# Graph network on one core: GpSimd multiplies out the left sides of two slots of each group, VectorE those of the other two

## The chip, the cores and the metric

The kernel runs on one core of one Trainium2 chip. The metric is the device time of the whole program in microseconds (us). The engines are TensorE (PE in the rows, PEld for its weight loads), VectorE (DVE), ScalarE (ACT), GpSimd (POOL) and SyncE (SP, which only issues DMAs).

## The reference, cut to what matters

512 nodes with 512 features pass four graph layers. The change lies in the preparation of the first, sparse attention over 8192 edges with eight heads:

```
p   = exp(q[row] . k[col] * scale + bias - m[row])      # per edge and head
out = segment_sum(p / segment_sum(p, row) * v[col], row)
```

The kernel does not gather per edge. It first builds dense tables: for each node `row`, each `col` and each head the sum of `exp(bias)` over the edges between them, and as a ninth table the number of these edges. The tables are made on TensorE as products of masks, and the attention is then dense.

## The kernel before, in words

The edges lie sorted by `dst`, in 64 tiles of 128 (an edge per partition). The destination nodes are cut into 37 blocks of 14 (`BW`). A **slot** is a tile together with a block that it meets; there is room for 100 slots (`SLOTS`), and four slots make a **group** (`GROUP`). For a slot, TensorE multiplies two things:

- the **left side**, 128 edges x 126: for each of the 14 nodes of the block and each of the nine columns (`KW`: eight heads and a one for the count) the edge's weight if it ends in that node, otherwise zero. It is `mask` (bf16, 14 wide) times `wp` (nine wide), both spread by broadcasting, and it is there twice, for a high and a low part of the weights (`a` = 0, 1). A group's left sides are 128 x 1008 numbers (4 slots x 2 parts x 126) in `st_ring`, which the rows show as `c_rounded`.
- the **one-hot**, 128 edges x 512: which node the edge comes from, `iota_f` compared with the edge's source, in `hot_ring`, which the rows show as `wide_rounded`.

Two matmuls a slot (128x126 by 128x512, line 1395) add into one of four accumulators in PSUM. `st_ring` and `hot_ring` hold `RING` = 2 groups.

Work on each engine is written out by hand in program order, and engines wait on semaphores. Groups 0 to 23 are unrolled, group 24 is a loop of `trips` rounds (one with these inputs, by the trace). Per group VectorE makes four one-hots (line 792), each waiting in `pair_mm` until TensorE has done with that slot two groups earlier, and then all left sides in one multiplication (line 798), which raises `built`. Behind some groups it also takes a finished tile of q, k or v out of PSUM (`qkv_out`, lines 817, 819, 823); behind group 3 it makes the later masks (line 757). TensorE takes group g once `built` has reached g + 1 (`pairs`), and between groups does 7, 4, 3, then ten times 2, then ten times 1 steps of the products for q, k and v (line 1377). ScalarE copies each finished block out of PSUM and clears the bank (lines 483, 488, semaphore `evacuated`). GpSimd fills constants in the first 9 us and does nothing after that.

Of the kernel before, what the change touches and what calls it, by code (L numbers as in the profile page):

```python
# [6 lines left out]
ALU = mybir.AluOpType  # L7
ACT = mybir.ActivationFunctionType
AX = mybir.AxisListType
F32 = mybir.dt.float32  # L10
# [6 lines left out]
P = 128  # L17
# [10 lines left out]
BW = 14  # L28
NBK = -(-N // BW)
KW = H + 1  # L30
# [6 lines left out]
GROUP = 4  # L37
NG = SLOTS // GROUP
RING = 2
ACC = 4  # L40
STAGES = 3
FIXED = SLOTS - GROUP
MAX_TRIPS = -(-(ET * NBK - FIXED) // GROUP)
FLOOR = -3e38
ENDS, PICK, NEEDS = 130, 200, 400
# [19 lines left out]
def gnn_kernel(nc, x, src, dst, bias, eps, cols, rows, wq, wk, wv, wo, w1_0, w2_0,  # L65
               wl_t, wr_t, w1_2, w2_2, w1_3t, w2_3t, out):
    ctx = ExitStack()
    with ctx:
# [75 lines left out]
        at, cuts = 0, {}  # L144
        for name, words in (("mask", SLOTS * BW), ("bias", HP * P), ("src", P), ("dst", P), ("low", P),
# [3 lines left out]
        mask = cuts["mask"].bitcast(BF16).rearrange("p (s a w) -> p s a w", a=2, w=BW)  # L149
# [18 lines left out]
        wp = wslot_r[:, 3, :, :].rearrange("p t n -> p (t n)")[:, 0:SLOTS * 2 * KW].rearrange(  # L168
            "p (s a k) -> p s a k", a=2, k=KW)
        st_ring = c1_r[:, :, :].rearrange("p t n -> p (t n)")[:, 0:RING * GROUP * 2 * BROWS].rearrange(  # L170
            "p (g a w k) -> p g a w k", g=RING, w=BW, k=KW)
# [42 lines left out]
        def rowp(name):  # L214
# [14 lines left out]
            "eps_column", "ln_var", "ln_std", "ln_coef", "h_ready", "z_ready",  # L229
            "bias_top", "bias_turned", "bias_column", "bias_spread", "bias_low", "lows_mm", "lows_ready", "weights_exp", "turned", "t_ready",  # L230
            "x_sums", "z_scalar", "w_hi", "pick_zeros", "meets_ready", "ranks_mm", "ranks_ready", "ends_mm", "ends_ready", "rounds_ready", "slots_ready", "slots_mm",
            "picks_ready", "rows_ready", "picks_mm", "weights_mm", "weights_read", "round_steps", "built", "pair_mm", "pair_steps",
            "evacuated", "staged", "b_out0", "b_out1", "b_out2", "c2_in", "qkv_mm",
            "qkv_ready",
            "c1_ready", "no_edge_ready", "bv_in", "b_ready", "qk_steps", "st_mm", "lows_found", "e_ready", "e_turned",
# [20 lines left out]
        LAST_V = range(3 * NT - 2, 3 * NT)  # L256
        assert qkv_group[NT * LAST_V[0] - 1] + RING < NG - 1
        chunk_w = bank[4][:, 0:H * GROUP]

        def block_parts(n):  # L260

            b = NBK - 1 - n
            if b == NBK - 1:
                return [((t, slice(TAKEN, P)), t * LEFT, LEFT) for t in range(NT)]
            first = b % BLOCKS
            return [((b // BLOCKS, slice(first, first + (BW - 1) * BLOCKS + 1, BLOCKS)), 0, BW)]
# [64 lines left out]
        @block.gpsimd  # L331
        def _(pool):
            nc.gpsimd.iota(steps[:, :], [[1, 1 + SLOTS]], base=0, channel_multiplier=0,
                           allow_small_or_imprecise_dtypes=True).then_inc(S["tables"], 1)
            nc.gpsimd.memset(ident[:, :], 0.0).then_inc(S["pool_order"], 1)
            nc.gpsimd.memset(ones[:, :], 1.0).then_inc(S["pool_order"], 1)
            pool.wait_ge(S["pool_order"], 2)
            nc.gpsimd.affine_select(out=ident[:, :], in_=ident[:, :], compare_op=ALU.not_equal, fill=1.0,
                                    base=0, pattern=[[-1, P]], channel_multiplier=1).then_inc(S["consts"], 1)

            nc.gpsimd.affine_select(out=before[:, :], in_=ones[:, :], compare_op=ALU.is_gt, fill=0.0,
                                    base=0, pattern=[[1, P]], channel_multiplier=-1).then_inc(S["consts"], 1)
            nc.gpsimd.iota(low_f, [[-BW, NBK + 1]], base=(NBK - 1) * BW, channel_multiplier=0,
                           allow_small_or_imprecise_dtypes=True).then_inc(S["tables"], 2)
            nc.gpsimd.iota(need_c[:, :], [[0, 1]], base=-NBK, channel_multiplier=1,
                           allow_small_or_imprecise_dtypes=True).then_inc(S["tables"], 1)
            nc.gpsimd.memset(pick, 0.0).then_inc(S["pick_zeros"], 1)
            nc.gpsimd.memset(wp[:, :, 0, H:].bitcast(F32), 1.0).then_inc(S["tables"], 1)
            nc.gpsimd.memset(wp[:, :, 1, H:].bitcast(F32), 0.0).then_inc(S["tables"], 1)
            pool.wait_ge(S["lows_ready"], 1)  # L350
            node_of = iota_f[:, :].rearrange("p (t c) -> p t c", t=NT)
            for t in range(NT):
                nc.gpsimd.iota(node_of[:, t, 0:TAKEN].rearrange("p (i j) -> p i j", j=BLOCKS),
                               [[1, BW], [BW, BLOCKS]], base=t * TAKEN, channel_multiplier=0,
                               allow_small_or_imprecise_dtypes=True).then_inc(S["tables"], 1)
            nc.gpsimd.iota(node_of[:, :, TAKEN:], [[LEFT, NT], [1, LEFT]], base=NT * TAKEN, channel_multiplier=0,
                           allow_small_or_imprecise_dtypes=True).then_inc(S["tables"], 1)
        @block.scalar
        def _(act):
            act.dma_start(idx_dst, dst.rearrange("(t p) -> t p", p=P)).then_inc(S["dst_in"], 16)  # L360
# [114 lines left out]
            for b in range(NBK):  # L475
# [3 lines left out]
                a = bank[(b + 1) % ACC][0:BROWS, :]  # L479
# [123 lines left out]
        def _(dve):  # L603
# [124 lines left out]
            def step(count, ins, wait=True):  # L728
                ins.then_inc(S["round_steps"], 1)
                if wait:  # L730
                    dve.wait_ge(S["round_steps"], count)
# [45 lines left out]
            whole, early = slice(0, SLOTS), slice(0, RING * GROUP)  # L777
            later, chunk = slice(RING * GROUP, SLOTS), slice(FIXED, SLOTS)
            next_masks, last_masks = slice(RING * GROUP, 6 * GROUP), slice(6 * GROUP, SLOTS)
# [7 lines left out]
            def one_hots(u, s0, ks=range(GROUP), freed=None):  # L787

                for k in ks:
                    if freed is not None:  # L790
                        dve.wait_ge(S["pair_mm"], freed + (k + 2))
                    nc.vector.tensor_scalar(hot_ring[:, u, k, :], iota_f[:, :], picked[:, 0, s0 + k:s0 + k + 1], None,  # L792
                                            ALU.is_equal)

            def left_sides(u, s0):

                c = slice(s0, s0 + GROUP)
                nc.vector.tensor_tensor(  # L798
                    st_ring[:, u, :, :, :],
                    mask[:, c, :, :].rearrange("p s a w -> p (s a) w").unsqueeze(3).broadcast_to(  # L800
                        [P, 2 * GROUP, BW, KW]),
                    wp[:, c, :, :].bitcast(F32).rearrange("p s a k -> p (s a) k").unsqueeze(2).broadcast_to(
                        [P, 2 * GROUP, BW, KW]), ALU.mult).then_inc(S["built"], 1)

            def build(g, u, s0, freed=None):

                one_hots(u, s0, freed=freed)
                left_sides(u, s0)

            def qkv_out(n):  # L810

# [36 lines left out]
            for t in (0, 1):  # L848
# [5 lines left out]
            step(8, slot_masks(next_masks))  # L854
            link(nc.vector.tensor_scalar(rounds_f[:, :], ends_row[:, NBK - 1:NBK], float(GROUP - 1 - FIXED),
                                         float(GROUP), ALU.add, ALU.max))
# [8 lines left out]
            dve.wait_ge(S["ends_ready"], 1)  # L865
            trips = dve.value_load(rounds_i[0:1, 0:1], min_val=1, max_val=MAX_TRIPS)
            for g in range(RING, NG - 1):
                build(g, g % RING, g * GROUP, (g - RING) * GROUP)
                if g == RING + 1:
                    step(9, slot_masks(last_masks))  # L870
                for n in range(LAST_V[0]):
                    if qkv_group[(n + 1) * NT - 1] + RING == g:
                        qkv_out(n)
            settle()
            with nc.vector.Fori(0, trips) as j:
                build(NG - 1, 0, FIXED, j * GROUP + (FIXED - RING * GROUP))
                at = j * 6 + 9
# [296 lines left out]
            for t in range(NT):  # L1174
                c = slice(t, t + 1)
# [13 lines left out]
        def _(pe):  # L1189
# [198 lines left out]
            def pairs(g, u, held):  # L1388

                pe.wait_ge(S["built"], g + 1)  # L1390
                for k in range(GROUP):
                    pe.wait_ge(S["evacuated"], held[k])
                    to = acc[0:BROWS, bass.ds((held[k] & (ACC - 1)) * N, N)]
                    for a in range(2):
                        last = nc.tensor.matmul(to, st_ring[:, u, 2 * k + a, :, :].rearrange("p w k -> p (w k)"),  # L1395
                                                hot_ring[:, u, k, :], start=False, stop=False, skip_group_check=True)
                    last.then_inc(S["pair_mm"], 1)
# [24 lines left out]
            for g in range(NG - 1):  # L1422
# [10 lines left out]
                if g == 2:  # L1433
                    pe.wait_ge(S["ends_ready"], 1)
                    trips = pe.value_load(rounds_i[0:1, 0:1], min_val=1, max_val=MAX_TRIPS)
            with nc.tensor.Fori(0, trips) as j:
                pe.wait_ge(S["rows_ready"], j + 1)
                pe.sem_inc(S["pair_steps"], 1)
                pairs(j + (NG - 1), 0, choices(FIXED))
                pe.wait_ge(S["qkv_ready"], LAST_V[0])  # L1440
                pair_table(j + 1, slice(FIXED, SLOTS), lambda k: qkv_step(len(qkv) - NT + k))

# [215 lines left out]
```

## Time and profile before

| what | us |
|---|---|
| median of three runs (393.72 to 393.85) | 393.78 |
| span of the profiled execution, first to last instruction | 394.1 |
| groups 0 to 24 and the q, k, v products on TensorE | 22 to 109.6 |
| TensorE busy in the whole span | 374.8 |
| VectorE busy | 312.1 |
| GpSimd busy | 4.2 |

The page gives no other time of the profiled execution than its span, which is 0.3 us above the median of the runs. Busy time counts instructions; where two of one engine overlap in the rows, the overlap counts once.

### The profile page before, as it was taken

To read this page: it belongs to the slowest core of one execution; us is meant where nothing else is said; L and a number is where in the kernel's file an instruction comes from. 1 tells how busy PE (TensorE), PEld (TensorE's weight loads), DVE (VectorE), ACT (ScalarE), POOL (GpSimd) and SP (SyncE) were. 2 spreads that over 40 slices of the span, in tenths; PEclk is the share of its full clock that TensorE was granted. 3 is DMA by queue.
4 is the path that set the end of the run, shared out by engine and by line. 5 is a ranking of instruction groups with operands and counts; after the bars stand their busy time and mean duration, and the time that the engine had idled before them with its cause. 6 is when DMAs were issued, how large, how long until landed. Compare 5 with 4: busy or idle time off the path is not lost.

```text
span 394.1 us, 5108 instructions
## 1 busy us (share of the span) xinstructions
PE 374.8 (95%) x1786; PEld 282.2 (72%) x1786; DVE 312.1 (79%) x660; ACT 171.6 (44%) x287; POOL 4.2 (1%) x19
## 2 busy tenths in 40 slices
PE   2989999999999999999999999999999999999994
PEld 1545566666657888887678788887588878787773
DVE  5889999999848789897868976698875788388236
ACT  5664666563044234244559533262363530145410
POOL 4000000000000000000000000000000000000000
PEclk9999999999999999999999999999999999999988
DMA  7602444343135000068200512200600050000002
GB/s 238 250 1 69 152 154 141 105 153 112 52 112 183 1 2 0 2 215 315 111 2 1 172 43 101 114 0 0 211 4 0 2 180 33 2 0 0 2 12 94
DMA packets 16360, 32.92 MB, mean 84 GB/s; under 512 B 1360, under 2 KB 1488, under 8 KB 16336
## 3 DMA queue, kind: packets, MB, share of 16 engines
q1 hardware_dynamic: 15744, 32.25, 23.9%
q10 hardware_dynamic: 592, 0.36, 0.3%
q8 instruction: 15, 0.25, 0.3%
q14 instruction: 9, 0.07, 0.1%
HBM read 21.07 MB, written 1.05 MB: 56 GB/s over the span
## 4 chain that ended last, share of the span: by engine, by line
PE 77%; DVE 14%; ACT 4%; issue 2%; DMA 1%; DVEq 0%; ACTq 0%
PE acc L1395 11%; PE bank L1377 10%; PE bank L1480 7%; PE bank L1270 6%; PE bank L1271 6%; PE bank L1251 4%; PE acc L1251 4%; PE acc L1271 4%; PE acc L1270 4%; PE bank L1465 3%; PE acc L1451 3%; DVE big_rounded L652 2%; PE acc L1228 2%; PE bank L1228 2%; PE acc L1545 2%
## 5 line engine op out<-in xcount | busy, mean ns | idle before, releaser
L1395 PE MATMUL acc<-wide_rounded,c_rounded 128*126 128x512 f32 x200 | 59.5, 439 | 0.7 <-ACT acc L464 0.7
L1395 PEld LDWEIGHTS acc<-wide_rounded,c_rounded 128*126 128x126 f32 x200 | 36.9, 186 | 19.8 <-issue 13.0
L792 DVE TENSOR_SCALAR wide_rounded<-iota_f,picked 128x512 fp32r<-128x512 f32 x100 | 42.2, 480 | 1.5 <-issue 1.1
L483 ACT COPY z_sb<-acc 126x512 f32<-126x512 f32 x37 | 21.6, 585 | 42.0 <-PE acc L1395 33.3
L507 ACT ACTIVATE wide<-wide,low_col 128x512 f32<-128x512 f32 x32 | 21.3, 715 | 32.9 <-DVE low_col L905 32.8
L1480 PEld LDWEIGHTS bank<-v_sb,big 128*128 128x128 f32 x256 | 29.7, 192 | 4.7 <-issue 4.0
L625 DVE TENSOR_TENSOR wslot_rounded<-wslot,wide_rounded 128x512 fp32r<-128x512 f32 x24 | 16.2, 687 | 21.2 <-ACT wslot L377 21.2
L1480 PE MATMUL bank<-v_sb,big 128*128 128x65 f32 x256 | 31.6, 277 | 0.0
L798 DVE TENSOR_TENSOR c_rounded<-row_bc,wslot_rounded 128x1008 fp32r<-128x1008 bf16 x25 | 30.0, 1201 | 0.0
L1377 PE MATMUL bank<-t_sb,wslot 128*128 128x512 f32 x64 | 29.5, 594 | 0.5 <-ACT t_sb L459 0.5
L652 DVE TENSOR_TENSOR big_rounded<-big,big_rounded 128x1024 fp32r<-128x1024 f32 x24 | 29.1, 1221 | 0.5
L369 ACT ACTIVATE std<-mv,eps_c 128x1 f32<-128x1 f32 x20 | 5.8, 290 | 41.0 <-DVE mv L657 25.9
L917 DVE TENSOR_TENSOR big<-bank,big 128x512 f32<-128x512 f32 x32 | 20.5, 682 | 0.9 <-PE bank L1465 0.9
L905 DVE CUSTOM_DVE_ANT_0 wide<-acc,t_sb 128x512 f32<-128x512 f32 x32 | 20.7, 683 | 0.2 <-DVE t_sb L893 0.2
L1377 PEld LDWEIGHTS bank<-t_sb,wslot 128*128 128x128 f32 x64 | 12.0, 189 | 11.5 <-issue 9.6
L488 ACT COPY acc<-zero_c 126x512 f32<-126x512 f32 x33 | 19.4, 588 | 1.0
L1271 PE MATMUL acc<-big_rounded,wslot_rounded 128*128 128x512 f32 x48 | 19.6, 409 | 0.0
L1270 PE MATMUL acc<-big_rounded,wide_rounded 128*128 128x512 f32 x48 | 19.4, 404 | 0.0
L1465 PE MATMUL bank<-ident,wide 128*128 128x128 f32 x128 | 17.6, 276 | 1.2 <-ACT wide L507 1.2
L1465 PEld LDWEIGHTS bank<-ident,wide 128*128 128x128 f32 x128 | 14.3, 146 | 3.1 <-ACT wide L507 2.5
L1377 PE MATMUL bank<-wslot,t_sb 128*128 128x512 f32 x32 | 16.4, 598 | 0.0
L374 ACT ACTIVATE wide_rounded<-bank,col 128x512 fp32r<-128x512 f32 x12 | 8.3, 693 | 17.4 <-PE bank L1271 17.4
(312 smaller groups left out, 769.6 us busy)
## 6 DMA issues: line engine op xcount, KB each, us to landing
big<-z_sb SPq DMA_DIRECT2D x36, 252.0 KB
big<-in_w SPq DMA_DIRECT2D x4, 2048.0 KB, 7.8
x_sb<-in_x SPq DMA_DIRECT2D x8, 256.0 KB, 4.6
big<-in_w_3t SPq DMA_DIRECT2D x2, 1024.0 KB, 6.7
row_bc<-in_rows SPq DMA_DIRECT2D x7, 256.0 KB, 6.4
wslot<-in_wq SPq DMA_DIRECT2D x1, 1024.0 KB, 8.9
wslot<-in_wk SPq DMA_DIRECT2D x1, 1024.0 KB, 10.7
wslot<-in_wv SPq DMA_DIRECT2D x1, 1024.0 KB, 12.8
```

The lines of the kernel that those rows point to most:

```text
L483: nc.scalar.copy(stage[0:BROWS, b % STAGES, :], a).then_inc(S["staged"], 1)
L507: nc.scalar.activation(e, e, ACT.Exp, bias=low_col[:, n // 4, h:h + 1], scale=-1.0).then_inc(S["e_ready"], 1)
L652: nc.vector.tensor_tensor(lo.rounded[:, part, :], lo.full[:, part, :], hi.rounded[:, part, :].bitcast(F32), ALU.subtract).then_inc(S[name ...
L792: nc.vector.tensor_scalar(hot_ring[:, u, k, :], iota_f[:, :], picked[:, 0, s0 + k:s0 + k + 1], None, ALU.is_equal)
L798: nc.vector.tensor_tensor(st_ring[:, u, :, :, :], mask[:, c, :, :].rearrange("p s a w -> p (s a) w").unsqueeze(3).broadcast_to([P, 2 * GRO ...
L1251: nc.tensor.matmul(bank[banks[m]][:, :], tile(a[0], m), r[0], start=(k == 0 and not started), stop=False)
L1270: nc.tensor.matmul(bank[b][:, :], tile(a[0], m), r[1], start=False, stop=False)
L1271: last = nc.tensor.matmul(bank[b][:, :], tile(a[1], m), r[0], start=False, stop=(k == len(terms) - 1))
L1377: ins = nc.tensor.matmul(to[:, :], left, right, start=(k == 0), stop=(k == NT - 1))
L1395: last = nc.tensor.matmul(to, st_ring[:, u, 2 * k + a, :, :].rearrange("p w k -> p (w k)"), hot_ring[:, u, k, :], start=False, stop=False, ...
L1465: last = nc.tensor.transpose(tile(bank[4 + a], t), tile(held_e[:, i % HELD, :], t), ident[:, :])
L1480: last = nc.tensor.matmul(o, by_head[:, t, h, m * P:(m + 1) * P], v_sb[:, t, h, :], start=(t == 0), stop=(t == NT - 1))
```

## The change

In groups 2 to 23 VectorE multiplies out the left sides of slots 0 and 1 only (`OWN = 2`), 128 x 504 instead of 128 x 1008. GpSimd multiplies out those of slots 2 and 3, also 128 x 504, from the same two tables. It waits until the masks are there (`round_steps`) and until TensorE is done with the whole group two before (`pair_mm`), and raises `built_pool`. TensorE waits for `built` before slot 0 as before, and for `built_pool` before slot 2. Groups 0, 1 and 24 stay with VectorE.

```diff
+OWN = 2
...
+        def sides(u, s0, first, n):
+
+            c = slice(s0 + first, s0 + first + n)
+            return (st_ring[:, u, 2 * first:2 * (first + n), :, :],
+                    mask[:, c, :, :].rearrange("p s a w -> p (s a) w").unsqueeze(3).broadcast_to([P, 2 * n, BW, KW]),
+                    wp[:, c, :, :].bitcast(F32).rearrange("p s a k -> p (s a) k").unsqueeze(2).broadcast_to(
+                        [P, 2 * n, BW, KW]))
...
+            pool.wait_ge(S["w_hi"], 2)
+            for g in range(RING, NG - 1):
+                if g in (RING, 6):
+                    pool.wait_ge(S["round_steps"], 8 if g < 6 else 9)
+                pool.wait_ge(S["pair_mm"], (g - RING) * GROUP + GROUP + 1)
+                to, at, by = sides(g % RING, g * GROUP, OWN, GROUP - OWN)
+                nc.gpsimd.tensor_tensor(to, at, by, ALU.mult).then_inc(S["built_pool"], 1)
...
+            def left_sides(u, s0, n=GROUP):
+
+                to, at, by = sides(u, s0, 0, n)
+                nc.vector.tensor_tensor(to, at, by, ALU.mult).then_inc(S["built"], 1)
+
+            def build(g, u, s0, freed=None, n=GROUP):
 
                 one_hots(u, s0, freed=freed)
-                left_sides(u, s0)
+                left_sides(u, s0, n)
...
-                build(g, g % RING, g * GROUP, (g - RING) * GROUP)
+                build(g, g % RING, g * GROUP, (g - RING) * GROUP, OWN)
...
                 pe.wait_ge(S["built"], g + 1)
                 for k in range(GROUP):
+                    if k == OWN and type(g) is int and g >= RING:
+                        pe.wait_ge(S["built_pool"], g - RING + 1)
```

VectorE around two groups of the first ten, before (L792 the one-hots, L798 the left sides, L817 and L819 the two halves of a `qkv_out`):

```order
L792 TENSOR_SCALAR wide_rounded<-iota_f,picked 128x512 [waits pair_mm] x4
L798 TENSOR_TENSOR c_rounded<-row_bc,wslot_rounded 128x1008
L817 TENSOR_SCALAR x_sb_rounded<-bank,col 128x512 [waits qkv_mm]
L819 SCALAR_TENSOR_TENSOR q_t_rounded<-bank,col,x_sb_rounded 128x512 [waits qk_steps]
L792 TENSOR_SCALAR wide_rounded<-iota_f,picked 128x512 [waits pair_mm] x4
L798 TENSOR_TENSOR c_rounded<-row_bc,wslot_rounded 128x1008
```

And in the changed kernel, where the same lines are L809, L815, L829 and L831:

```order
L809 TENSOR_SCALAR wide_rounded<-iota_f,picked 128x512 [waits pair_mm] x4
L815 TENSOR_TENSOR c_rounded<-row_bc,wslot_rounded 128x504
L829 TENSOR_SCALAR x_sb_rounded<-bank,col 128x512 [waits qkv_mm]
L831 SCALAR_TENSOR_TENSOR q_t_rounded<-bank,col,x_sb_rounded 128x512 [waits qk_steps]
L809 TENSOR_SCALAR wide_rounded<-iota_f,picked 128x512 [waits pair_mm] x4
L815 TENSOR_TENSOR c_rounded<-row_bc,wslot_rounded 128x504
```

No instruction moved on VectorE; the multiplication is half as wide.

GpSimd at the end of its program, before (the last constants, then the end):

```order
L347 MEMSET row_bc 128x200
L348 MEMSET wslot_rounded 128x100
L349 MEMSET wslot_rounded 128x100
L353 IOTA iota_f 128x126 [waits lows_ready]
L353 IOTA iota_f 128x126 x3
L356 IOTA iota_f 128x4x2
L68 UNCONDITIONAL_BRANCH
```

And in the changed kernel, where these lines are L356 to L365:

```order
L358 MEMSET wslot_rounded 128x100
L362 IOTA iota_f 128x126 [waits lows_ready]
L362 IOTA iota_f 128x126 x3
L365 IOTA iota_f 128x4x2
L373 TENSOR_TENSOR c_rounded<-row_bc,wslot_rounded 128x504 [waits pair_mm,round_steps,w_hi]
L373 TENSOR_TENSOR c_rounded<-row_bc,wslot_rounded 128x504 [waits pair_mm] x3
L373 TENSOR_TENSOR c_rounded<-row_bc,wslot_rounded 128x504 [waits pair_mm,round_steps]
L373 TENSOR_TENSOR c_rounded<-row_bc,wslot_rounded 128x504 [waits pair_mm] x17
L69 UNCONDITIONAL_BRANCH
```

22 multiplications are new there; nothing stands behind them.

TensorE in one group, from the second slot to the third, before:

```order
L1395 REGISTER_ALU [waits evacuated]
L1395 ISA
L1395 MATMUL acc<-wide_rounded,c_rounded 126x512 x2
L1395 REGISTER_ALU [waits evacuated]
L1395 ISA
L1395 MATMUL acc<-wide_rounded,c_rounded 126x512 x2
```

And in the changed kernel, from group 2 on (the line is now L1409):

```order
L1409 REGISTER_ALU [waits evacuated]
L1409 ISA
L1409 MATMUL acc<-wide_rounded,c_rounded 126x512 x2
L1409 REGISTER_ALU [waits evacuated,built_pool]
L1409 ISA
L1409 MATMUL acc<-wide_rounded,c_rounded 126x512 x2
```

The third slot has one more wait; the order of the matmuls is the same.

## Rows read from the trace of the kernel before

**Rows 1.** Busy time of each engine by stretch, us from the span's start.

```profile
core 0: us, PE busy (x) PEld busy (x) DVE busy (x) ACT busy (x) POOL busy (x), PEclk, DMA share, GB/s
32.00:77.00 45.00, 45.00 (x151) 27.87 (x149) 44.36 (x76) 25.15 (x44) 0.00 (x0) 1.00 0.42 133
77.00:107.00 30.00, 30.00 (x111) 20.22 (x110) 29.89 (x56) 12.26 (x21) 0.00 (x0) 1.00 0.33 106
```

**Rows 2.** The chain that ended last, in order of time: start, us, what.

```profile
59.45 1.84 PE acc L1395 x8
...
63.01 1.85 PE acc L1395 x8
...
80.00 1.86 PE acc L1395 x8
...
85.44 1.84 PE acc L1395 x8
...
88.14 1.87 PE acc L1395 x8
...
90.87 2.04 PE acc L1395 x8
...
101.90 1.97 PE acc L1395 x8
...
104.73 3.97 PE acc L1395 x16
```

**Rows 3.** VectorE's waits from 29 to 107 us: total, times, longest.

```profile
DVE wide_rounded L792 <- PE acc L1395: 0.2, 1, 0.2
```

**Rows 4.** The timeline of VectorE in the late groups: start, us, what.

```profile
76.80 1.20 DVE L798 TENSOR_TENSOR c_rounded<-row_bc,wslot_rounded 128x1008 fp32r<-128x1008 bf16 x1
...
85.60 1.20 DVE L798 TENSOR_TENSOR c_rounded<-row_bc,wslot_rounded 128x1008 fp32r<-128x1008 bf16 x1
86.72 1.67 DVE L792 TENSOR_SCALAR wide_rounded<-iota_f,picked 128x512 fp32r<-128x512 f32 x4
88.31 1.20 DVE L798 TENSOR_TENSOR c_rounded<-row_bc,wslot_rounded 128x1008 fp32r<-128x1008 bf16 x1
...
105.12 1.21 DVE L798 TENSOR_TENSOR c_rounded<-row_bc,wslot_rounded 128x1008 fp32r<-128x1008 bf16 x1
```

**Rows 5.** Groups of VectorE's instructions from 29 to 107 us: count, busy us, mean ns.

```profile
L819 DVE SCALAR_TENSOR_TENSOR q_t_rounded<-bank,col,x_sb_rounded 128x512 fp32r<-128x512 f32 x4 | 3.0, 752 | 0.1
L817 DVE TENSOR_SCALAR x_sb_rounded<-bank,col 128x512 fp32r<-128x512 f32 x4 | 3.0, 746 | 0.0
```

**Rows 6.** The attention's timeline: two VectorE multiplications of 128x512, start and us.

```profile
119.06 1.28 DVE L917 TENSOR_TENSOR big<-bank,big 128x512 f32<-128x512 f32 x2
```

**Rows 7.** Groups of GpSimd's instructions in the whole span, costliest kinds.

```profile
L353 POOL IOTA iota_f<- 128x126 f32 x4 | 1.9, 531 | 3.7 <-DVE row_bc L694 3.7
L341 POOL TENSOR_SCALAR_AFFINE_SELECT before<-ones 128x128 f32<-128x128 f32 x1 | 0.3, 295 | 0.0
```

**Rows 8.** Timeline of GpSimd and VectorE in the first 9 us: start, us, what.

```profile
2.25 0.75 DVE L680 COPY slot<-rcnt_sb 128x100 f32<-128x100 f32 x1 [1.19 <-POOL z_sb L343]
2.27 0.26 POOL L347 MEMSET row_bc<- 128x200 f32 x1
2.38 0.64 DVE L681 TENSOR_SCALAR z_sb<-z_sb 64x37 f32<-64x37 f32 x1
2.59 0.34 POOL L349 MEMSET wslot_rounded<- 128x100 f32 x1
...
4.02 0.22 DVE L683 CAST row_bc<-z_sb 64x128 f32<-64x128 int32 x1 [1.00 <-DMA z_sb<-in_dst]
4.78 0.24 DVE L686 TENSOR_SCALAR z_sb<-z_sb,tops 64x37 f32<-64x37 f32 x1
...
6.59 1.93 POOL L353 IOTA iota_f<- 128x126 f32 x4 [3.66 <-DVE row_bc L694]
7.67 0.46 DVE L713 CAST row_bc<-z_sb 64x128 f32<-64x128 int32 x1
```

More of the change, by code:

```diff
@@ L231, in gnn_kernel @@
             "x_sums", "z_scalar", "w_hi", "pick_zeros", "meets_ready", "ranks_mm", "ranks_ready", "ends_mm", "ends_ready", "rounds_ready", "slots_ready", "slots_mm",
-            "picks_ready", "rows_ready", "picks_mm", "weights_mm", "weights_read", "round_steps", "built", "pair_mm", "pair_steps",
+            "picks_ready", "rows_ready", "picks_mm", "weights_mm", "weights_read", "round_steps", "built", "built_pool", "pair_mm", "pair_steps",
             "evacuated", "staged", "b_out0", "b_out1", "b_out2", "c2_in", "qkv_mm",
@@ L793, in one_hots @@
                                             ALU.is_equal)
[L795 to L805, printed above, removed]
+            def left_sides(u, s0, n=GROUP):
+                to, at, by = sides(u, s0, 0, n)
+                nc.vector.tensor_tensor(to, at, by, ALU.mult).then_inc(S["built"], 1)
+            def build(g, u, s0, freed=None, n=GROUP):
                 one_hots(u, s0, freed=freed)
-                left_sides(u, s0)
+                left_sides(u, s0, n)
             def qkv_out(n):
```

## The prediction, made before the changed kernel ran

> **What bounds the kernel now.** I read the busy time by stretch first. Between 32 and 77 us, and again between 77 and 107, TensorE is busy all the time at a granted clock of 1.00, which is its upper level of 2.4 GHz; but VectorE is busy for 44.4 of 45.0 and 29.9 of 30.0 us too [rows 1]. Two engines are full, so the question is which of them waits for the other. The chain that ended last answers it: in this stage it runs over TensorE alone, eight matmuls of a group (1.84 to 1.87 us), then the steps for q, k and v, then the next group [rows 2]. From one group's start to the next it is 3.56 us early (59.45 to 63.01) and 2.70 us late (85.44 to 88.14; over the ten groups from 14 at 80.00 to 24 at about 106.6 it is 2.7 on average). VectorE for its part waited for TensorE once, for 0.2 us [rows 3]. So VectorE never rests and yet is never late: the left sides of group 14 are done at 78.00 for a start at 80.00, those of group 24 at 106.33 for a start at 104.73 + 1.85 = 106.58 [rows 2, 4]. It starts 2 us ahead and ends 0.25 us ahead. TensorE is the bound, VectorE is next, by a hair.
>
> **What there is to gain.** Nearly nothing, since TensorE's own work does not change. Against a plain 1.85 us a group, the groups at 90.87, 101.90 and 104.73 (the last a double one, against 3.70) took 0.19, 0.12 and 0.27 us more [rows 2]; if all of it were lateness of VectorE, 0.6 us would come back. That is less than 0.2% of 393.8 us (0.8 us), which is about what a measurement of this kernel can tell from no change.
>
> **What is taken from VectorE.** In a late group it starts the left sides at 85.60, the one-hots at 86.72 and the next left sides at 88.31 [rows 4]: 1.12 us for 1008 elements, 1.59 us for four one-hots, 2.71 in all. The half as wide multiplication has 504 elements a partition; the nearest row is a multiplication of 512, two of which take 1.28 us with their overlap, so 0.60 us from start to start with a last one of 0.68 [rows 6]. The change takes off 1.12 - 0.60 = 0.52 us a group and leaves 1.59 + 0.60 = 2.19 us.
>
> **What is put on GpSimd.** 22 multiplications of 504 elements, of a kind that the trace does not show on that engine. From below: the select, its only row that reads and writes SBUF, does 128 elements in 0.295 us, and these follow each other every 0.25; four times that is 1.0 us for 504 elements with one input read [rows 7]. From above: the iota does 126 elements in 0.531 us, and 504 would take 2.1 us [rows 7]. The multiplication is nearer to the select, but reads two inputs where that reads one; I take 1.2 us.
>
> The Trainium skill (GPSIMD Engine Reference, section 3.1) says that two inputs share one read port there and gives 4497 ns for a multiplication's sister, an addition of 2048 fp32 elements. By an estimate from that page it would be 1.1 us here, and the time below would come to 401; no run here shows it.
>
> Taken by itself this is hidden. GpSimd may start when group g - 2 is done, and slot 2 of group g comes after one set of steps, the group g - 1, another set and two slots: the steps take what a period has beside the group, 0.86 us late (2.70 - 1.84) and 1.72 early, so late 0.86 + 1.85 + 0.86 + 0.92 = 4.5 us and early 6.2 us [rows 2].
>
> **What the two engines do to each other.** This decides the case, and the trace of before has a place for it, at the very start. A VectorE comparison of 64 x 37 takes 0.24 us at 4.78, with GpSimd idle; the same shape takes 0.64 us at 2.38, while GpSimd is in its memsets. The copy of 128 x 100 beside it takes 0.75 us. Both end 0.07 to 0.09 us after the last memset, which ends at 2.59 + 0.34 = 2.93 [rows 8]. It is seen a second time: the cast of 64 x 128 takes 0.22 us at 4.02 and 0.46 us at 7.67, inside GpSimd's iotas [rows 8]. So some VectorE instructions between SBUF tensors do not run beside a GpSimd instruction, they wait for its end. The one-hots are of that kind: they read and write SBUF, with 512 elements in about 0.40 us each (1.59 for four) [rows 4], while the same 512 elements out of PSUM take 0.746 us [rows 5]. That the left sides are of that kind as well, the trace does not show; I take it that they are, since they too read two tables in SBUF.
>
> The Trainium skill (SBUF — State Buffer, "Who interferes with whom") states the rule: VectorE and GpSimd share one pair of SBUF ports, which one holds for a whole instruction while the other waits; a VectorE instruction takes it when it moves one tensor over both ports or has two inputs in SBUF. The rows at the start agree for the first kind, and nothing in this trace speaks to the second. By this rule the sum is the one that follows; without it the time would be the first rival's.
>
> **The sum.** If they exclude each other, a group needs 1.59 + 0.60 us of VectorE and 1.2 us of GpSimd one after the other, and two handovers. A handover costs the overlap that neighbours on VectorE have now (1.20 - 1.12 = 0.08 us [rows 4]) or the 0.07 to 0.09 us after the last memset; I take 0.1 each. Together 1.59 + 0.60 + 1.20 + 0.20 = 3.59 us.
> - Early groups: 3.59 against TensorE's 3.56, so nothing lost, if the `qkv_out` instructions, which read PSUM (0.75 us each, two every other group [rows 5]), run beside GpSimd. If they never do, a group costs 0.72 us more, some 6.5 us over nine groups.
> - Late groups: 3.59 against 2.71 for ten periods, from group 14 to group 24: 10 x 0.88 = 8.8 us. VectorE's lead of up to 2.0 us takes some of it; it would be smaller by then, and I take off 0.6. So 8.2 us.
> - Group 24 has no GpSimd part, and what follows is a chain on TensorE that starts later by the same amount; nothing in it makes up for that.
>
> The waits come to stand on TensorE: before slot 0, at `built`, or before slot 2, at `built_pool`. Behind them on that engine are the q, k, v steps and everything else. Against the profiled span the sum is 394.1 + 8.2 = 402.3 us, and against the median of the runs, which lies 0.3 lower, **402.0 us**.
>
> By the bounds of the multiplication: with 1.0 us a group takes 3.39 us, the late groups lose 0.68 each, and the time is 393.8 + 6.2 = 400.0. With 2.1 us it takes 4.49: 0.93 lost in nine early groups and 1.78 in ten late ones, 8.4 + 17.8 - 0.6 = 25.6, so 419.4. With 1.5 us it is 0.33 x 9 + 1.18 x 10 - 0.6 = 14.2, so 408.0.
>
> **Rivals.**
> - *They run side by side.* The memsets and iotas that the rows show only write; a multiplication that reads might get along with VectorE. Then 1.2 us is well inside 4.5, VectorE gains 0.52 us a group that nobody waits for, and the time stays at 393.8, or 393.2 with the 0.6 us from above. This is the side where it is not slower; it holds as long as VectorE's 2.19 us plus whatever contention adds stays under 2.71 us. What speaks against it are the two stalls at the start.
> - *Only the one-hots exclude GpSimd.* Then 1.59 + 1.20 + 0.20 = 2.99 us must follow each other, 0.28 above 2.71: 2.8 us over ten late groups, less the lead of up to 2: 394.6 to 396.6.
> - *GpSimd is slow.* Broadcast operands with runs of nine elements, and one in bf16, are unlike the select. At the iota's rate it is the 419.4 worked out above.
>
> **How the numbers follow.** Exclusion with 1.0 to 1.6 us a multiplication, 398 to 411 us by the terms above: 0.60. Exclusion with a slower one, up to 419.4 and a little beyond: 0.12. Exclusion with the one-hots alone, or in part, 394.6 to 398: 0.10. Side by side, within 0.8 us of 393.8: 0.15. Faster by more than that: 0.03, since only 0.6 us can be seen to gain. The range from 394.6 to 419.5 holds about 0.80: it leaves out the side by side case and faster (0.18) and a tail at the slow end. Slower has 0.60 + 0.12 + 0.10 = 0.82, same 0.15, faster 0.03.
>
> **What the profile after would show.** GpSimd with 22 multiplications of 128 x 504 of about 1.2 us. VectorE's one-hots no longer evenly 480 ns, some stretched by about a GpSimd instruction. In the chain, VectorE and GpSimd pieces in between TensorE's groups; groups 3.6 us apart from 77 us on, and hardly changed before it. After the groups the same rows as before, some 8 us later. The prediction is wrong if one-hots keep their 480 ns while GpSimd works (then the time is unchanged), if GpSimd's multiplications take 2 us or more (then the early groups stretch as well), or if the early groups stretch at 1.2 us, which would say that the `qkv_out` instructions give no cover.

## The result, and the profile after

The changed kernel takes 395.91 us (median of 9 runs, 395.63 to 396.50) against 393.85 us for the kernel before beside it: 1.0042 times as long, with a 95% interval of 1.0027 to 1.0056. It is slower by some 2 us, where 8 were forecast. Runs of the kernel before fall on two levels 1.7 us apart (393.5 to 394.3 and 395.2 to 395.9), as do those of other kernels, in shares that differ from one series to the next, so a difference called "like for like" below is one between medians of the lower level alone. Like for like the change costs 2.1 us. The two profiled spans (394.1 and 394.8) are only 0.7 us apart; in the last 24 us that of before had a granted clock of 0.86 and that of after one of 0.98.

The stretches after, in the columns of [rows 1]:

```profile
32.00:77.00 45.00, 45.00 (x152) 27.95 (x150) 44.59 (x72) 25.21 (x44) 13.75 (x12) 1.00 0.42 134
77.00:107.00 30.00, 29.09 (x105) 18.93 (x104) 30.00 (x55) 12.24 (x21) 10.87 (x9) 1.00 0.32 105
```

Up to 77 us TensorE is as full as before. After that it has gaps, 0.9 us up to 107 and more behind it, while VectorE is full to the end. The clock is 1.00 in both stretches, so it has no part in this. The chain that ended last now runs over VectorE (start, us, what):

```profile
32.51 2.29 DVE wide_rounded L809 x4
...
78.34 0.59 DVE c_rounded L815
...
87.95 2.40 DVE wide_rounded L809 x4
90.36 0.59 DVE c_rounded L815
90.95 2.40 DVE wide_rounded L809 x4
93.34 0.59 DVE c_rounded L815
...
96.94 0.60 DVE v_sb L835
97.54 1.80 DVE wide_rounded L809 x4
...
107.50 1.13 DVE c_rounded L815
108.63 0.23 issue
108.86 2.11 PE acc L1409 x8
```

From 32.5 us to the end of the left sides of group 24 no other engine's work stands in this chain. A late group takes 2.40 + 0.59 = 2.99 us of VectorE, against 2.71 in [rows 4]. The left sides of group 24 end at 108.6, where they ended at 106.33, 2.3 us later; this is what arrives at the end. What became of the one-hots is seen in the timeline of the two engines:

```profile
87.88 0.47 DVE L809 TENSOR_SCALAR wide_rounded<-iota_f,picked 128x512 fp32r<-128x512 f32 x1
88.02 1.26 POOL L373 TENSOR_TENSOR c_rounded<-row_bc,wslot_rounded 128x504 fp32r<-128x504 bf16 x1 [2.13 <-PE acc L1409]
88.27 1.29 DVE L809 TENSOR_SCALAR wide_rounded<-iota_f,picked 128x512 fp32r<-128x512 f32 x1
...
90.28 0.67 DVE L815 TENSOR_TENSOR c_rounded<-row_bc,wslot_rounded 128x504 fp32r<-128x504 bf16 x1
90.75 1.13 POOL L373 TENSOR_TENSOR c_rounded<-row_bc,wslot_rounded 128x504 fp32r<-128x504 bf16 x1 [1.46 <-PE acc L1409]
90.87 1.29 DVE L809 TENSOR_SCALAR wide_rounded<-iota_f,picked 128x512 fp32r<-128x512 f32 x1
92.08 0.47 DVE L809 TENSOR_SCALAR wide_rounded<-iota_f,picked 128x512 fp32r<-128x512 f32 x1
```

One one-hot in most late groups takes 1.29 us in place of 0.48: it is held for 0.81 us. The others keep their length. (Where a `qkv_out` stands before the one-hots, as `v_sb` does at 96.94, the hold is smaller, and the four take 1.80 us in place of 2.40.) At 90.87 the held one-hot ends at 92.16; with 0.48 us of its own it went on at 91.68, and GpSimd's multiplication is recorded until 91.88. It lets go 0.2 us before its recorded end. The first one begins inside a one-hot, waits for it (1.26 us in place of 1.07), and the next one-hot is held for the same 0.81 us.

All multiplications of GpSimd, with shortest, median and longest in ns:

```profile
L373 POOL TENSOR_TENSOR c_rounded<-row_bc,wslot_rounded x22: 1067/1132/1409, 26.5 to 102.4; 128x504 fp32r<-128x504 bf16 x22
```

### The profile page after: what moved, and what is told of

Read it like the earlier page. It is cut to its first block, busy times and chain, and to the rows that moved or that the text cites. A ratio compares the mean times of both kernels' runs of the same rounds, so it can differ in the third digit from the quotient of the medians.

```text
span 394.8 us, 5154 instructions
## 1 busy us (share of the span) xinstructions
PE 373.7 (95%) x1786; PEld 280.7 (71%) x1786; DVE 314.6 (80%) x660; ACT 171.7 (43%) x287; POOL 29.8 (8%) x41
## 4 chain that ended last, share of the span: by engine, by line
PE 58%; DVE 33%; ACT 4%; issue 3%; DMA 1%; ACTq 0%; DVEq 0%
DVE wide_rounded L809 13%; PE bank L1494 7%; PE bank L1282 6%; PE bank L1283 6%; PE bank L1263 4%; PE acc L1263 4%; PE acc L1282 4%; PE acc L1283 4%; PE bank L1479 3%; DVE c_rounded L815 3%; PE acc L1465 3%; PE bank L1389 2%; DVE big_rounded L669 2%; PE acc L1240 2%; PE bank L1240 2%
## 5 line engine op out<-in xcount | busy, mean ns | idle before, releaser
L1409 PE MATMUL acc<-wide_rounded,c_rounded 128*126 128x512 f32 x200 | 58.4, 433 | 2.1 <-issue 0.9
L809 DVE TENSOR_SCALAR wide_rounded<-iota_f,picked 128x512 fp32r<-128x512 f32 x100 | 55.6, 613 | 1.4 <-issue 1.1
L1409 PEld LDWEIGHTS acc<-wide_rounded,c_rounded 128*126 128x126 f32 x200 | 36.7, 186 | 22.0 <-issue 15.2
L373 POOL TENSOR_TENSOR c_rounded<-row_bc,wslot_rounded 128x504 fp32r<-128x504 bf16 x22 | 25.7, 1168 | 69.7 <-PE acc L1409 51.7
L1283 PE MATMUL acc<-big_rounded,wslot_rounded 128*128 128x512 f32 x48 | 18.7, 389 | 0.0
L815 DVE TENSOR_TENSOR c_rounded<-row_bc,wslot_rounded 128x504 fp32r<-128x504 bf16 (+1 forms) x25 | 18.4, 735 | 0.0
```

The lines of the kernel that those rows point to most:

```text
L373: nc.gpsimd.tensor_tensor(to, at, by, ALU.mult).then_inc(S["built_pool"], 1)
L815: nc.vector.tensor_tensor(to, at, by, ALU.mult).then_inc(S["built"], 1)
L1283: last = nc.tensor.matmul(bank[b][:, :], tile(a[1], m), r[0], start=False, stop=(k == len(terms) - 1))
```

## The experiments

Theory 1: GpSimd's multiplication holds VectorE up for 0.81 us, this alone costs time, and it does so to the left sides as much as to the one-hots. Theory 2: TensorE comes late because slot 2 waits for GpSimd. And the second rival of the prediction: the left sides run beside GpSimd, and only the one-hots are held. Its 2.99 us a group is the number that was measured, so it needs a test of its own.

**Only the part that takes work off VectorE.** From the changed kernel (GpSimd's loop and its waits go with the multiplication):

```diff
-                nc.gpsimd.tensor_tensor(to, at, by, ALU.mult).then_inc(S["built_pool"], 1)
...
-                    if k == OWN and type(g) is int and g >= RING:
-                        pe.wait_ge(S["built_pool"], g - RING + 1)
```

> Only the part that takes work off VectorE: it multiplies out slots 0 and 1 in groups 2 to 23, GpSimd does nothing, and TensorE uses what lies in the ring for slots 2 and 3 (their left sides are left out, so the tables are wrong). All theories: TensorE is the bound, so 393.8 us, at best 0.6 less; VectorE then waits for the ring for some 0.5 us a late group, with 2.19 us of work in 2.71. If it came out above 394.6, neither GpSimd nor its wait would be needed to explain the loss.

Measured: 394.14 us (12 runs, lowest 393.14), 0.9990 of before (0.9971 to 1.0009). The three groups that took 2.04, 1.97 and 3.97 us in [rows 2] (the last a double one) take 1.86, 1.86 and 3.72 in the chain that ended last:

```profile
90.56 1.86 PE acc L1399 x8
...
101.43 1.86 PE acc L1399 x8
103.29 0.86 PE bank L1381 x2
104.15 3.72 PE acc L1399 x16
```

Over all runs the interval does not tell half the left sides from nothing. Like for like it is 0.54 us less (393.22 against 393.76), and the three groups give back 0.18 + 0.11 + 0.25 = 0.54 us: nearly all of the 0.6 us that the prediction read from the chain.

So VectorE was a little late in the kernel before, though up to group 23 its left sides were done about 1 us or more before TensorE's matmuls came to them. The trace of before shows by what way for group 18. TensorE's instruction queue runs ahead of its matmuls: its wait for VectorE's left sides of group 17 ends with them, at 86.8, and at 87.7 it begins to read the row numbers of the next two groups (`rows_u`), which takes 2.63 us, to 90.34. The first weights of group 18 are loaded behind that, at 90.78:

```profile
L1383 PEldq TENSOR_LOAD <-rows_u x1: 2632/2632/2632, 87.7 to 87.7; - x1
...
90.78 0.76 PEld L1395 LDWEIGHTS acc<-wide_rounded,c_rounded 128*126 128x126 f32 x4 [0.75 <-issue]
```

In the run without the other half the same read begins at 86.4. No run changed the read by itself.

**GpSimd works, nobody uses it.** The product goes to a spare row of `z_sb`, TensorE does not wait (left out of the cut, here and in the next runs of this kind: GpSimd waits for its own last product, and VectorE, behind all groups, for GpSimd's last):

```diff
-                nc.gpsimd.tensor_tensor(to, at, by, ALU.mult).then_inc(S["built_pool"], 1)
+                nc.gpsimd.tensor_tensor(z_sb_r[:, NT - 1, 0:504].rearrange("p (a w k) -> p a w k", w=BW, k=KW), at, by, ALU.mult).then_inc(S["built_pool"], 1)
...
-                        pe.wait_ge(S["built_pool"], g - RING + 1)
```

> As the changed kernel, but GpSimd writes its products to a spare place, TensorE doesn't wait for them and uses what lies in the ring for slots 2 and 3. Theory 1 (a GpSimd multiplication holds up one VectorE one-hot by 0.81 us, and nothing else costs): the same 395.9 us as the changed kernel, a late group of VectorE 2.99 us. Theory 2 (TensorE comes late because slot 2 waits for GpSimd): 393.8 us.

Measured: 396.04 us (12 runs), 1.0048 (1.0031 to 1.0065), like for like 2.1 us more than before (395.88 against 393.76): the whole loss is there without any wait of TensorE for GpSimd. Its chain, over the last groups, is VectorE's again:

```profile
105.57 1.66 DVE wide_rounded L811 x4
107.23 1.12 DVE c_rounded L817
108.36 0.23 issue
108.58 2.10 PE acc L1410 x8
```

Theory 2 falls.

**One slot, and three slots, for GpSimd.** `OWN = 3`, and `OWN = 1`.

> OWN = 3: GpSimd makes one slot's left sides (252 elements), VectorE three (756). If the hold is in proportion to the elements (0.81 us for 504, so 0.41): a late group of VectorE takes 1.59 + 0.86 + 0.41 = 2.86 us, 0.15 above 2.71, ten times less a lead of 0.6: 394.7 us. If half of the hold is fixed (0.41 + 0.20): 3.06 us, 396.7.

> OWN = 1: GpSimd makes three slots' left sides (756 elements), VectorE one (252, 0.34 us). In proportion: 1.59 + 0.34 + 1.22 = 3.15 us a late group, 0.44 above 2.71: 4.4 - 0.6, so 397.6 us. With half of the hold fixed (0.41 + 0.61): 2.95 us, 395.6. If TensorE's wait for GpSimd mattered, GpSimd's 1.6 us would show in it here more than with two slots.

Measured: 395.13 us (12 runs), 1.0022 (1.0004 to 1.0041), with one slot; 399.56 us (6 runs), 1.0118 (1.0091 to 1.0145), with three. Before had a median of 395.28 us beside them, so the medians can't be compared as they stand. Like for like one slot costs 1.2 us (394.99 against 393.76), where the proportional hold said 0.9 and the half fixed one 2.9; three slots cost 4.5 us (the two lowest of six runs, 398.3), where it said 3.8. The timeline with one slot:

```profile
87.32 2.04 DVE L809 TENSOR_SCALAR wide_rounded<-iota_f,picked 128x512 fp32r<-128x512 f32 x4
89.28 0.93 DVE L815 TENSOR_TENSOR c_rounded<-row_bc,wslot_rounded 128x756 fp32r<-128x756 bf16 x1
90.13 2.03 DVE L809 TENSOR_SCALAR wide_rounded<-iota_f,picked 128x512 fp32r<-128x512 f32 x4
...
87.25 0.63 POOL L373 TENSOR_TENSOR c_rounded<-row_bc,wslot_rounded 128x252 fp32r<-128x252 bf16 x1 [2.18 <-PE acc L1409]
```

And with three:

```profile
89.14 2.93 DVE L809 TENSOR_SCALAR wide_rounded<-iota_f,picked 128x512 fp32r<-128x512 f32 x4
92.00 1.72 DVE L815 TENSOR_TENSOR c_rounded<-row_bc,wslot_rounded 128x252 fp32r<-128x252 bf16 x1
93.64 1.66 DVE L809 TENSOR_SCALAR wide_rounded<-iota_f,picked 128x512 fp32r<-128x512 f32 x4
95.22 0.40 DVE L815 TENSOR_TENSOR c_rounded<-row_bc,wslot_rounded 128x252 fp32r<-128x252 bf16 x1
...
91.85 1.59 POOL L373 TENSOR_TENSOR c_rounded<-row_bc,wslot_rounded 128x756 fp32r<-128x756 bf16 x1 [0.85 <-PE acc L1409]
```

Four one-hots take 1.96 us with one slot on GpSimd (87.32 to 89.28), held by 1.96 - 1.59 = 0.37. With three, the left sides at 92.00 take 1.72 us in place of 0.40, held by 1.32; GpSimd had begun at 91.85. So left sides are held just as one-hots are (those at 89.14 by 2.86 - 1.59 = 1.27), which by the second rival could not be. The hold is 0.37, 0.81 and 1.32 us for 252, 504 and 756 elements, 0.44 and 0.51 a further slot, while the same 252 elements cost VectorE (1.12 - 0.60) / 2 = 0.26 us. Each slot that moves costs VectorE more than it saves.

**GpSimd's work in addition.** The product unused as above, and VectorE makes all left sides:

```diff
-                build(g, g % RING, g * GROUP, (g - RING) * GROUP, OWN)
+                build(g, g % RING, g * GROUP, (g - RING) * GROUP)
```

> VectorE makes all left sides as in the kernel before; GpSimd does its 22 multiplications of 504 elements all the same, into a spare place, and nobody waits for them. A doubling of the suspected cost alone. Theory 1: a late group of VectorE takes 1.59 + 1.12 + 0.81 = 3.52 us, 0.81 above 2.71, and the early ones 0.5 us above TensorE's 3.56: 8.1 + 4.3 less a lead of 1 to 2, some 404.5 us. Theory 2 (waiting for GpSimd's product): 393.8, since nobody waits.

Measured: 403.99 us (4 runs), 1.0236 (1.0203 to 1.0268). The timeline has the expected 3.52 us a group (85.22 to 88.74), and shows the other direction of the exclusion:

```profile
84.10 1.20 DVE L817 TENSOR_TENSOR c_rounded<-row_bc,wslot_rounded 128x1008 fp32r<-128x1008 bf16 x1
85.22 2.48 DVE L811 TENSOR_SCALAR wide_rounded<-iota_f,picked 128x512 fp32r<-128x512 f32 x4
87.62 1.20 DVE L817 TENSOR_TENSOR c_rounded<-row_bc,wslot_rounded 128x1008 fp32r<-128x1008 bf16 x1
88.74 0.68 DVE L837 TENSOR_TENSOR v_sb<-bank,row_bc 128x512 f32<-128x512 f32 x1
...
84.20 2.02 POOL L375 TENSOR_TENSOR z_sb_rounded<-row_bc,wslot_rounded 128x504 fp32r<-128x504 bf16 x1 [1.50 <-PE acc L1410]
```

GpSimd becomes ready 0.1 us into the left sides and takes 2.02 us in place of 1.07: it waits for their end, and then holds a one-hot for the same 0.81 us.

**The same, begun behind the one-hots.** GpSimd waits for a mark on the group's fourth one-hot in place of `pair_mm`:

```diff
-                pool.wait_ge(S["pair_mm"], (g - RING) * GROUP + GROUP + 1)
+                pool.wait_ge(S["hots"], g - RING + 1)
...
+                if done:
+                    last.then_inc(S["hots"], 1)
```

> As the one with extra work (VectorE makes all, GpSimd's product unused), but GpSimd starts when VectorE has made the group's four one-hots, so that it meets the left sides (1.12 us) first. If left sides and GpSimd exclude each other: GpSimd's multiplications grow from 1.07 to about 2 us, since they wait for the end of the left sides, the next one-hot is stretched as before, and the time is near 404. If the left sides run beside it: 1.07 us, left sides 1.20, one-hots stretched by 0.3 at most, some 396 us.

Measured: 405.98 us (4 runs), 1.0273 (1.0238 to 1.0308). All 22 multiplications meet the left sides and last 1.96 us in the mean:

```profile
L375 POOL TENSOR_TENSOR z_sb_rounded<-row_bc,wslot_rounded 128x504 fp32r<-128x504 bf16 x22 | 43.1, 1960 | 62.9 <-DVE wide_rounded L811 62.9
```

The left sides stay at 1.20 us, so they and GpSimd exclude each other whichever comes first. Like for like it is 0.5 us slower than the run above (its lowest run, 404.53, against 403.99); the making of the later masks (line 757 of before) is held here too, 3.24 us in place of 2.37, which is enough for that.

**GpSimd only writes.** An iota of 504 elements stands in place of the multiplication, with the left sides as in the second experiment:

```diff
-                nc.gpsimd.tensor_tensor(to, at, by, ALU.mult).then_inc(S["built_pool"], 1)
+                nc.gpsimd.iota(z_sb[:, NT - 1, 0:504], [[1, 504]], base=0, channel_multiplier=0,
+                               allow_small_or_imprecise_dtypes=True).then_inc(S["built_pool"], 1)
```

> VectorE makes slots 0 and 1 only; instead of its multiplication GpSimd runs an iota of 504 elements into a spare place, which reads nothing (slots 2 and 3 use what lies in the ring, the tables are wrong). If only GpSimd's reading holds up VectorE: one-hots at 480 ns, 393.8 us. If writing does as well, as at the start of the program: one one-hot in each group stretched by about the iota's length, which is 1.9 us at the rate of the iotas of before, a late group of 4.1 us, some 412 us; with an iota as long as the multiplication, about 396.

Measured: 393.39 us (10 runs), 0.9983 (0.9963 to 1.0004). The time says nothing on its own, since the iota is much shorter than I took it to be; the timeline does:

```profile
88.79 2.01 DVE L812 TENSOR_SCALAR wide_rounded<-iota_f,picked 128x512 fp32r<-128x512 f32 x4
90.72 0.66 DVE L818 TENSOR_TENSOR c_rounded<-row_bc,wslot_rounded 128x504 fp32r<-128x504 bf16 x1
...
89.96 0.55 POOL L375 IOTA z_sb<- 128x504 f32 x1 [1.97 <-PE acc L1411]
```

The iota lasts 0.55 us, and four one-hots take 1.93 us (88.79 to 90.72), held by 0.34. So an instruction that only writes holds the one-hots as well. A group is then 1.93 + 0.59 = 2.52 us, still under 2.71, and nothing is lost; like for like it is 0.5 us less than before (393.35 against 393.84), as without GpSimd. Whether it would hold the left sides was not seen.

**The split in the early groups alone.** `SPLIT = range(RING, 13)` in the loops of GpSimd and VectorE and in TensorE's condition.

> The split in groups 2 to 12 only, where TensorE needs 3.56 us a group; the late groups as in the kernel before. Theory 1: the early groups of VectorE take 2.99 us and a qkv_out that covers part of GpSimd's work, about TensorE's pace, and VectorE comes to the late ones with a lead of 1 to 2 us as before: 393.8 to 394.6 us. If the early groups carried part of the loss: above that, towards 395.9.

Measured: 394.30 us (12 runs), 1.0011 (0.9993 to 1.0030), which does not tell it from before; like for like it is 0.4 us more (394.27 against 393.84). TensorE is at 45.00 of 45.0 us up to 77 and at 29.71 of 30.0 after it: the early groups cost it nothing while they last, but VectorE comes out of them with less of its lead. Most of the loss is not there, and no split there gains any. With TensorE the bound and 0.54 us all that came back when half the left sides were simply gone, no split tried here beats the kernel before.

## Why the prediction was right in sign and wrong in size

- **TensorE is the bound and VectorE next to it.** Right: with half the left sides gone, 0.9990 of before, like for like 0.54 us of the 0.6 that it named. That VectorE "is never late" holds for TensorE's matmuls alone, not for its instruction queue (first experiment).
- **0.52 us a group comes off VectorE.** Right: 0.59 us for 504 elements where 0.60 was forecast.
- **GpSimd's multiplication takes 1.2 us**, between 1.0 and 2.1. Right: 1.07 when it meets nothing, 1.13 in the median.
- **The two engines exclude each other, one-hots and left sides alike.** Right, and shown in both directions: a left side held for 1.32 us, a multiplication kept waiting for 0.9 (1.96 in place of 1.07). The rule of the Trainium skill (SBUF — State Buffer, "Who interferes with whom") names both kinds, and these runs agree with it; the hold is shorter than the instruction, though (next point).
- **"Together 1.59 + 0.60 + 1.20 + 0.20 = 3.59 us."** This is the step that failed. I put the whole length of GpSimd's multiplication into the sum, and two handovers of 0.1 us. Measured is a hold of 0.81 us with everything in it: 1.59 + 0.81 + 0.59 = 2.99. The two mistakes are 0.39 us (1.20 against 0.81) and 0.20 us a group, and over ten late groups they are the 6 us between forecast and result. With 2.99 the prediction's own sum gives 0.28 x 10 - 0.6 = 2.2 us, and 396.0 us in place of 402.0, against 395.91 measured. That it comes so close is in part luck, for its other terms are not what the trace has. The left sides of group 14 end at 78.93 (before at 78.00), those of group 24 at 108.6 (before at 106.33): the late groups add 1.4 us and not 2.8, because in two of the ten a `qkv_out` covers most of GpSimd's work and group 24 has none of it; and 0.93 us stands there at group 14 already (next point). A row stood there that could have told me: in [rows 8] a comparison that lasts 0.24 us by itself ended only 0.09 us after the last memset, so it began 0.15 us before the memset's recorded end.
- **Early groups lose nothing because `qkv_out` covers.** Right for TensorE, which is full up to 77 us; with 2.99 us there was also less to cover than with 3.59. Not right for VectorE: it is busy for 44.59 of 45.0 us here, so what it is held for is missing from its lead at group 14, 0.93 us (of which 0.15 was there at 32 us already). The 0.4 us of the split in the early groups alone fits this.
- **The rival with the one-hots alone** named 394.6 to 396.6 us, where the time lies. Its mechanism is not the one at work: its 2.99 us was the same sum for another reason, a full 1.20 + 0.20 us that would have fallen on the one-hots alone. The held left side with three slots settles it.

The measured time lies inside the range, but in the part that the prediction gave to exclusion "with the one-hots alone, or in part" at 0.10; the change is a quarter of the one forecast.

## What to carry to other kernels

Before work is handed from one engine to another, read what the two do to each other, then price the handover by how long one holds the other up, not by how long the handed instruction lasts; a place where an instruction of known length ends just behind the other engine's gives that time. Where a slot's work costs the first engine 0.26 us and holds it up for 0.4 us when the second does it, no number of slots helps; one, two and three all lost. And two engines at 100% do not make both the bound: taking half the left sides off the one that is hardly waited for was worth 0.54 us here.

## What the hardware did that I had not expected

- GpSimd's multiplication of broadcast operands, one of them bf16, took 0.62, 1.07 and 1.51 us for 252, 504 and 756 elements where it met nothing, close to the select's rate in [rows 7], and held VectorE up for 0.2 to 0.3 us less than that (0.37, 0.81, 1.27 to 1.32).
- An iota of 504 elements in one run took 0.55 us, hardly more than those of 126 elements in [rows 7] (0.531), whose numbers are made in 14 runs of nine.
- A VectorE instruction that was in progress when GpSimd became ready lengthened GpSimd's instruction (1.26, 1.41, 2.02 us), not its own; the next one was held for the same 0.81 us.
